# Opening of a retention block: query weights split ahead of key weights, one reduction and one statistics step moved, three fillers taken out

## The reference

```
mod = silu(c) @ wmod              -> sa, ca, ga, sb, cb, gb
ga, gb: sign kept, absolute value at least 0.25
h = layernorm(x) * (1 + ca) + sa
q, k = rotary(h Wq), rotary(h Wk)        8 heads of 64
v = h Wv (8 heads of 128);  g = h Wg
scores = q k^T / 8 * decay, causal;  o = scores v
o = groupnorm(o per head) * w + b, times silu(g);  x = x + ga * (o Wo)
h = layernorm(x) * (1 + cb) + sb
x = x + gb * ffn(h)     r = sigmoid(xr W_r), k = relu(xk W_k)^2, r * (k W_v), with token shift
```

## Time and profile before

| | us |
|---|---|
| median of 3 runs | 750.47 (750.15 to 750.76) |
| the profiled execution | 750.22 |
| its span, first to last instruction | 748.4 |
| TensorE busy | 737.4 |
| VectorE busy | 600.5 |
| GpSimd busy | 589.0 |
| ScalarE busy | 490.2 |

### The profile page before, as it was taken

The page is one execution under the profiler, slowest core; times in us unless marked ns, Lnnn a source line. Parts: engine busy times, 40 slices in busy tenths (PEclk is TensorE's granted clock), DMA queues, the critical chain, the costliest instruction groups (busy, mean ns, idle before and its releaser), DMA issues.

```text
span 748.4 us, 29033 instructions
## 1 busy us (share of the span) xinstructions
PE 737.4 (99%) x12159; PEld 648.3 (87%) x12159; DVE 600.5 (80%) x1265; ACT 490.2 (65%) x956; POOL 589.0 (79%) x643
## 2 busy tenths in 40 slices
PE   8989999999999999999999999999999999999997
PEld 7778888888988888888888988888888988988886
DVE  4997787978788787987879798797987878787546
ACT  4566667676675766767666666756667576656665
POOL 6877788888789887898878888788877988787641
PEclk9999999999999999999999999999999999999999
DMA  6611000001011010111102011020111101001100
GB/s 249 193 31 19 13 17 17 16 18 31 12 27 39 10 44 16 24 37 31 31 10 51 16 24 32 13 48 17 28 26 31 34 14 31 16 9 31 24 16 28
DMA packets 56161, 25.67 MB, mean 34 GB/s; under 512 B 36184, under 2 KB 53856, under 8 KB 56032
## 3 DMA queue, kind: packets, MB, share of 16 engines
q1 hardware_dynamic: 55312, 23.02, 12.9%
q10 hardware_dynamic: 720, 0.80, 0.3%
HBM read 11.22 MB, written 4.20 MB: 21 GB/s over the span
## 4 chain that ended last, share of the span: by engine, by line
PE 92%; DVE 3%; ACT 1%; issue 1%; DMA 1%; POOL 1%; SPq 0%; DVEq 0%
PE ring L309 52%; PE outs L309 15%; PE O_E L309 14%; PE ring L324 8%; PE O_O L309 3%; PE ring L374 2%; DMA N<-in_w_vT 1%; ACT y L771 0%; DVE N L1097 0%; DVE rot_k L1060 0%; DVE A L1070 0%; DVE qT L1031 0%; DVE sin_k L1063 0%; POOL gn_rstd L1383 0%; DVE ln_stats L1004 0%
## 5 line engine op out<-in xcount | busy, mean ns | idle before, releaser
L1390 POOL TENSOR_TENSOR y<-y,gate 128x512 f32<-128x512 f32 x120 | 154.8, 1308 | 29.5 <-ACT y L771 29.5
L735 ACT ACTIVATE v<-ring 64x512 f32<-64x512 f32 x128 | 75.9, 593 | 85.6 <-PE ring L309 84.8
L1373 POOL TENSOR_TENSOR rot_k<-rot_k,sin_k 128x256 f32<-128x256 f32 x128 | 106.8, 856 | 24.1 <-DVE sin_k L1063 24.1
L309 PEld LDWEIGHTS outs<-wo_gated,y 128*128 128x128 f32 x992 | 119.7, 192 | 5.1 <-DVE y L1136 0.5
L309 PE MATMUL outs<-wo_gated,y 128*128 128x128 f32 x992 | 121.7, 275 | 0.1
L1090 DVE TENSOR_REDUCE gn_sum<-N 128x4 f32<-128x512 f32 x118 | 75.5, 681 | 42.4 <-ACT N L759 42.4
L1383 POOL TENSOR_TENSOR gn_rstd<-gn_var,minus_half 128x8 f32<-128x8 f32 x64 | 105.3, 1645 | 5.0
L1070 DVE TENSOR_TENSOR A<-ring,consts 128x256 f32<-128x256 f32 x128 | 47.9, 415 | 60.1 <-PE ring L309 60.1
L771 ACT ACTIVATE y<-ring,gn 128x512 f32<-128x512 f32 x126 | 90.8, 775 | 5.2 <-PE ring L324 5.2
L1367 POOL TENSOR_TENSOR qT<-qT,swapped 128x512 f32<-128x512 f32 x60 | 76.9, 1282 | 18.1 <-DVE swapped L1046 17.8
L743 ACT ACTIVATE kT<-ring 128x512 f32<-128x512 f32 x64 | 38.2, 597 | 80.1 <-PE ring L324 80.1
(11 more groups left out here) (193 smaller groups left out, 2100.8 us busy)
## 6 DMA issues: line engine op xcount, KB each, us to landing
k_odd<-rot_k SPq DMA_DIRECT2D x128, 64.0 KB, 2.4
X<-in_x SPq DMA_DIRECT2D x16, 256.0 KB, 3.9
out<-X SPq DMA_DIRECT2D x15, 256.0 KB, 2.5
key_tables<-in_const SPq DMA_DIRECT2D x7, 256.0 KB, 5.5
rotary_q<-in_const_q SPq DMA_DIRECT2D x2, 512.0 KB, 6.4
gates<-stored_rows SPq DMA_DIRECT2D x8, 128.0 KB, 3.2
N<-in_w_qkT SPq DMA_DIRECT2D x1, 512.0 KB, 5.1
N<-in_w_vT SPq DMA_DIRECT2D x1, 512.0 KB, 6.3
```

The costliest lines, as they stand in the source:

```text
L309: return e.matmul(o, lhsT, rhs, start=start, stop=stop, skip_group_check=True)
L735: done = e.activation(v[halves(half), i % 2, 1, :, :], by(PAIRS, bank_of["v", odd, i][halves(1 - half), :]), ACT.Copy)
L1373: done = e.tensor_tensor(turned[:, n, :, :], turned[:, n, :, :], sin[:, n, :, :], op)
L1390: e.tensor_tensor(y[:, n % NY, :], y[:, n % NY, :], gate[:, n % 2, :], ALU.mult).then_inc(sem["y"])
```

## The change

The one semaphore step of the query and key weights becomes two: ScalarE rounds the query half, then (after the partners) the key half; GpSimd's low parts go in the same order. On VectorE `sum_w_v` moves behind `low_h(0)`. The query pair's own semaphore now comes after three matmuls and the partners' after six; VectorE takes the cosine product first. The last pair's subtraction moves from GpSimd to VectorE. Three fillers ahead of `scores(0)` go. On VectorE `norm_stats(2, 0)` moves behind `rotate_q(6)`; GpSimd's list keeps its order there. The tables of chunks 4 to 7 share one semaphore, which is waited for as a whole.

```diff
 TensorE
-                split_matmul(bank[:, :], [wqk[s][:, cols] ...], h_parts(0))
+                split_matmul(bank[:, :], [wqk[s][:, cols] ...], h_parts(0)).then_inc(sem["proj_q"])
                 at.wait_ge("w_partners_lo", 1)
                 at.wait_ge("sin_q", p - 1)
                 bank = bank_of["q_partners", p] = O[p % 2][:, :, :].rearrange("p n v -> p (n v)")
-                split_matmul(bank, [mix_k[s][:, cols] ...], h_parts(0)).then_inc(sem["proj_q"])
+                split_matmul(bank, [mix_k[s][:, cols] ...], h_parts(0)).then_inc(sem["proj_partners"])
 project_k:
-                at.wait_ge("w_qk_lo", 1)
+                at.wait_ge("w_qk_lo", 2)
             transpose_k(0)
             project_v(1, 1)
-            keep_busy(out_bank, 3, True)
             scores(0)
 ScalarE
-            at.wait_ge("w_qk", 16)
-            split_w("w_qk", raw_qk, wqk)
+            round_w_qk(0)
             norm_apply(0, 0)
             round_w_partners()
+            round_w_qk(1)
+            round_h(0)
             scale_v_mean()
-            round_h(0)
             round_w_v(1)
 VectorE
             norm_stats(0, 0)
-            sum_w_v()
             mod_columns()
             full_h(0)
             low_h(0)
+            sum_w_v()
             rotate_q_pair(0)
...
             add_state(2)
+            rotate_q(6)
             norm_stats(2, 0)
-            rotate_q(6)
             rotate_k(4)
 rotate_q_pair on VectorE:
                 at.wait_ge("proj_q", p + 1)
+                e.tensor_tensor(q, bank_of["q", p][:, :], rotary_q[:, 0, 0:W], ALU.mult).then_inc(sem["cos_q"])
+                at.wait_ge("proj_partners", p + 1)
                 at.wait_ge("qT", p - 1)
+                e.tensor_tensor(partners, bank_of["q_partners", p], rotary_q[:, 1, 0:W], ALU.mult).then_inc(sem["sin_q"])
+                if p == PAIRS - 1:
+                    at.wait_ge("cos_q", PAIRS)
+                    at.wait_ge("sin_q", PAIRS)
+                    e.tensor_tensor(q, q, partners, ALU.subtract).then_inc(sem["qT"])
 GpSimd
-            split_w_qk()
+            low_w_qk(0)
             low_w_partners()
+            low_w_qk(1)
             centre_w_v(1)
...
             rotate_q(2)
-            rotate_q(3)
             rotate_k(1)
```

More of the change, by code:

```diff
@@ L39 @@
 NORM_AHEAD = 4
+EARLY_TABLES = 4
 SEMAPHORES = (
@@ L53 @@
     "silu_c", "sin_k", "sin_q", "small_consts", "sq_E", "sq_O", "state", "sum_E", "sum_O",
-    "swapped", "tables0", "tables1", "tables2", "tables3", "tables4", "tables5", "tables6", "tables7", "v_E",
+    "swapped", "tables0", "tables1", "tables2", "tables3", "late_tables", "v_E",
     "v_O", "v_mean", "v_sum", "w_ffn", "w_g", "w_g_hi", "w_g_lo", "w_k_hi", "w_k_lo",
-    "w_mod", "w_o", "w_qk", "w_qk_hi", "w_qk_lo", "w_v", "w_v_centred", "w_v_hi", "w_partners_hi", "w_partners_lo", "w_v_lo", "wffn_v",
+    "w_mod", "w_o", "w_qk", "w_qk_hi", "w_qk_lo", "w_v", "w_v_centred", "w_v_hi", "proj_partners", "w_partners_hi", "w_partners_lo", "w_v_lo", "wffn_v",
     "wo_gated", "x0", "x1", "x2", "x3", "x4", "x5", "x6", "y", "zero_column",
@@ L257, in outs, with halves_of_w, tables @@
             return [banks[j // PJ][:, j, :] for j in range(GC)]
+        def halves_of_w(n):
+            return slice(n * H * D, (n + 1) * H * D)
         def gates_of(b):
             return "gates%d" % (b % 2), 16 * (b // 2 + 1)
+        def tables(c):
+            return ("tables%d" % c, 16) if c < EARLY_TABLES else ("late_tables", 16 * (CB - EARLY_TABLES))
         def loaded(g):
@@ L348, in project_q_pair @@
                 at.wait_ge("hT_lo", 1)
-                split_matmul(bank[:, :], [wqk[s][:, cols] for s in ("hi", "lo")], h_parts(0))
+                split_matmul(bank[:, :], [wqk[s][:, cols] for s in ("hi", "lo")], h_parts(0)).then_inc(sem["proj_q"])
                 at.wait_ge("w_partners_lo", 1)
@@ L352, in project_q_pair @@
                 bank = bank_of["q_partners", p] = O[p % 2][:, :, :].rearrange("p n v -> p (n v)")
-                split_matmul(bank, [mix_k[s][:, cols] for s in ("hi", "lo")], h_parts(0)).then_inc(sem["proj_q"])
+                split_matmul(bank, [mix_k[s][:, cols] for s in ("hi", "lo")], h_parts(0)).then_inc(sem["proj_partners"])
             def warm_up(n):
@@ L696, in split_w, with round_w_qk @@
                 e.activation(parts["hi"][:, :], raw_w, ACT.Copy).then_inc(sem[name + "_hi"])
+            def round_w_qk(keys):
+                cols = halves_of_w(keys)
+                at.wait_ge("w_qk", 16)
+                e.activation(wqk["hi"][:, cols], raw_qk[:, cols], ACT.Copy).then_inc(sem["w_qk_hi"])
             def scale_v_mean():
@@ L748, in square @@
                 if i < GC:
-                    at.wait_ge(*(("w_partners_lo", 1), ("w_g_lo", 1), ("w_v_centred", 2), ("w_v_lo", 2))[i])
+                    at.wait_ge(*(("w_qk_lo", 2), ("w_g_lo", 1), ("w_v_centred", 2), ("w_v_lo", 2))[i])
                 at.wait_ge("nT_psum", PAIRS * ((i - NN) // GC + 1))
@@ L812, in load_tables @@
                 columns = const[:, n_const + c * H * D:n_const + (c + 1) * H * D]
-                e.dma_start(key_tables[:, c, :, :, :].rearrange("p k h d -> p (k h d)"), columns).then_inc(sem["tables%d" % c], 16)
+                e.dma_start(key_tables[:, c, :, :, :].rearrange("p k h d -> p (k h d)"), columns).then_inc(sem[tables(c)[0]], 16)
             def last_apply(part):
@@ L1024, in rotate_q_pair @@
             def rotate_q_pair(p):
+                q, partners = qT[:, 0, p, :], (turned, swapped)[p % 2][:, :]
                 at.wait_ge("const_q0", 16)
                 at.wait_ge("proj_q", p + 1)
+                e.tensor_tensor(q, bank_of["q", p][:, :], rotary_q[:, 0, 0:W], ALU.mult).then_inc(sem["cos_q"])
+                at.wait_ge("proj_partners", p + 1)
                 at.wait_ge("qT", p - 1)
-                e.tensor_tensor((turned, swapped)[p % 2][:, :], bank_of["q_partners", p], rotary_q[:, 1, 0:W], ALU.mult
-                                ).then_inc(sem["sin_q"])
-                e.tensor_tensor(qT[:, 0, p, :], bank_of["q", p][:, :], rotary_q[:, 0, 0:W], ALU.mult).then_inc(sem["cos_q"])
+                e.tensor_tensor(partners, bank_of["q_partners", p], rotary_q[:, 1, 0:W], ALU.mult).then_inc(sem["sin_q"])
[3 more added lines that the diff above has]
+                    e.tensor_tensor(q, q, partners, ALU.subtract).then_inc(sem["qT"])
             def rotate_q(m):
@@ L1049, in rotate_k @@
                 c, bank = i % CB, bank_of["k", i]
-                at.wait_ge("tables%d" % c, 16)
+                at.wait_ge(*tables(c))
                 at.wait_ge("proj_k", i + 1)
@@ L1321, in norm_rstd, with low_w_qk @@
                                 ).then_inc(sem[f"ln_shift{which}"])
-            def split_w_qk():
-                at.wait_ge("w_qk_hi", 1)
-                e.tensor_tensor(wqk["lo"][:, :], raw_qk, wqk["hi"][:, :].bitcast(F32), ALU.subtract).then_inc(sem["w_qk_lo"])
+            def low_w_qk(keys):
+                cols = halves_of_w(keys)
+                at.wait_ge("w_qk_hi", keys + 1)
+                e.tensor_tensor(wqk["lo"][:, cols], raw_qk[:, cols], wqk["hi"][:, cols].bitcast(F32), ALU.subtract
+                                ).then_inc(sem["w_qk_lo"])
             def low_w_partners():
```

## The result

| | before | after |
|---|---|---|
| median, 6 runs each | 750.17 us | 754.11 us (752.50 to 754.24) |
| the profiled execution | 750.22 | 754.16 |
| its span | 748.4 | 752.4 |

The ratio is 1.0045 (95% interval 1.0034 to 1.0055): slower, and 1.1 us above the forecast range.

The account below looks back on a forecast made before the run. TensorE was taken as the bound, 99% busy, with the opening at VectorE's pace. The statistics move, 1.81 less a 0.48 us lead, gave +1.33 on 750.22: 751.55, or 751.8 as median; forecast 751.5 to 752.1, range 749.9 to 753.0.

Parts of the forecast that it names:

- the lead at the statistics: VectorE, ahead of `norm_stats(2, 0)`: 0.48 us earlier than before, to be taken off the 1.81 us step.
- the clock: Rival: TensorE falls to 1.2 GHz for the twelve projection matmuls behind the new gap; +4.3 us, 754.8; chance 0.05.
- The large term: `norm_stats(2, 0)` behind `rotate_q(6)` delays GpSimd's chain to `norm_heads(1, 0)`: 1.81 less 0.48 of lead, +1.33 us.
- The lead of 1.22 us has shrunk to 0.2 us: VectorE's lead at `low_w_v(1)`, mostly held up by GpSimd's chain and the subtract, leaves 0.2 us at `rotate_k(1)`.
- Lead at that point: 0.48 us: VectorE starts the mask of chunk 2 at 37.24 instead of 37.72; ends 0.2 and 0.75 us.
- 0.4 for a VectorE operation beside it: Opening: GpSimd's key-half subtraction, ending near 12.0, was allowed 0.4 us extra for a VectorE operation beside it.
- a share: GpSimd's extra 0.46 and 0.44 us beside VectorE operations of 0.82 and 0.72 were read as only part of them.
- 752.4 by the rule: Under whole exclusion GpSimd would lose 1.54 us, 0.64 more; the sum becomes 1.33 + 0.64, 752.4 us.
- Edits at nothing: Late tables on one semaphore, `square(0)` waiting for the key half and fewer semaphores: cost 0.
- The other side: Rival: opening lead survives in full, 1.90 us against 1.81, so -0.1 us, 750.4; chance 0.13.

Follow-up runs that it names:

- e5: e1 with GpSimd's low part of the key half made to wait for `hT_lo`; 750.08 us, ratio 0.9990 to the kernel before.
- e7: e1 with `sum_w_v` ahead of `mod_columns` again on VectorE; 750.30 us, ratio 0.9997 to the kernel before.
- e6: e1 with the last pair's subtraction on GpSimd again; 750.29 us, ratio 0.9995 to the kernel before.
- e1: Changed kernel with `norm_stats(2, 0)` back ahead of `rotate_q(6)` on VectorE; 750.91 us, ratio 1.0007 to the kernel before.
- e2: Kernel before with only `norm_stats(2, 0)` moved behind `rotate_q(6)` on VectorE; 753.59 us, ratio 1.0046 to the kernel before.
- e4: Changed kernel with the matmuls of `state(3)` issued three times, giving TensorE work in the gap; 752.81 us, ratio 1.0034 to the kernel before.
- f1: e1 with both GpSimd's key half waiting for `hT_lo` and the last pair's subtraction on GpSimd; 749.52 us, ratio 0.9988 to the kernel before.
- f2: f1 with 5 instead of 9 fillers between the first transposes and `project_q_pair(0)`; 749.42 us, ratio 0.9993 to the kernel before.
- e3: Changed kernel with `head_rstd(1)` ahead of `norm_rstd(2, 0)` in GpSimd's list; 751.30 us, ratio 1.0012 to the kernel before.

## Why the prediction was wrong

Its place and its mechanism of loss were right, its size was not. Two terms failed: the lead at the statistics, forecast as +0.48 us and measured as -0.92, and the clock, which was left out of the sum with a chance of 0.05 and cost 1.45 us. The forecast for one execution was 751.55; with the 1.40 and the 1.45, and 0.2 less for the pause near 75 us, it comes to 754.2, and 754.16 was measured.

- **The large term** held: 1.81 was 1.82, the chain of 3.57 us was 3.57, the idle spot of 2.5 us was 2.43 (before the clock).
- **"The lead of 1.22 us has shrunk to 0.2 us"** failed, with "Lead at that point: 0.48 us". The lead was -1.22 us at `rotate_k(1)` and -0.92 at the statistics. This step failed one part earlier, where GpSimd's key half is allowed "0.4 for a VectorE operation beside it" and `low_h(0)` nothing: I let VectorE always win. It was VectorE that waited, 0.88 us at `low_h(0)` (1.57 against 0.69), 0.74 at `low_w_v(1)` (1.56 against 0.82) under GpSimd's `rotate_q(0)`, of which only the last 0.26 us had lain there before the later centring moved it, and 0.3 more at the gate rows (1.30 against 1.01) under `low_h(1)`. e5 shows the first by taking it away. The second was not taken away by itself, but `low_w_v(1)` took only 0.71 and 0.70 us in the executions of e5 and e7 in which GpSimd's `rotate_q(0)` was nearly over when it started.
- **The -1.22 us in full**: ahead of `low_w_v(1)` the lead was 0.17 (16.03 against 16.20) where 1.22 was forecast, 0.88 of the difference by `low_h(0)` and 0.16 because `full_h(0)` started at 9.16 and not at 9.00. Then come -0.74 in `low_w_v(1)`, +0.14 for the wait ahead of pair 3 that went, and -0.79 for the subtraction and the pause of 0.18 before it. The subtraction had been priced at 0.1, because VectorE was thought to wait for GpSimd there in any case. VectorE was too late for that, and e6 gives 0.82 us at `rotate_k(1)` back.
- **The rule and the row.** The prediction set "a share" against the Trainium skill's whole exclusion (SBUF — State Buffer, "Who interferes with whom"). The trace agrees with the page after all: GpSimd's `rotate_k(0)` began at 16.42 while `low_w_v(1)` ran until 17.02, 0.6 us, and took 0.46 longer. What is lost is the rest of the operation that started first, not the whole of it, and either engine can be the loser. The rows fit this closely, with the loss 0.13 to 0.15 us below the rest: 0.60 gave 0.46, and 0.57 gave 0.44 (GpSimd, before); 1.03 gave 0.88 (`low_h(0)`, after) and 1.17 gave 1.03 (the same in e1); rests of 0.15 and 0.16 gave 0.01 or less (`low_w_v(1)` in e7 and e5, against 0.70 undisturbed). The "752.4 by the rule" priced GpSimd's losses alone. That VectorE can lose stood in the trace before: the last gate product took 1.01 us beside GpSimd's `low_h(1)`, where others of its size took 0.40. The kernel before:

```profile
30.15 0.40 DVE L984 SCALAR_TENSOR_TENSOR gate_rows<-outs,gate_rows 8x256 f32<-8x256 f32 x1
30.59 1.01 DVE L987 TENSOR_TENSOR gate_rows<-gate_pos,gate_rows 8x256 f32<-8x256 f32 x1
30.05 1.27 POOL L1347 TENSOR_TENSOR hT_lo<-h_full,hT_hi 128x512 fp32r<-128x512 f32 x1
```

- **The clock** was a rival with 0.05, priced at +4.3 with the whole twelve projections at 1.2 GHz. It came, with six of the twelve and the transposes behind them slow, and took 1.3 to 1.45 us. Its price in 754.8 was too high, and that the measured 754.11 lies near this rival's time is luck: a price too high met a lead that was not there. The chance was too low because the row it leaned on, no fall across 1.12 us of idle time, says nothing of twice as much: the clock fell after 2.08 us in e2 and 2.39 us in the changed kernel, and not after 0.92 us in e4.
- **Edits at nothing** held: no row after shows a wait for the late tables. The scores of chunk 0 started at 22.68, earlier than before (23.44) but not at 21.5.
- **The other side**, a lead of 1.9 us, had no part in it. Even f1, with one of the blocks taken away and the subtraction back on GpSimd, leads by 0.87 at `rotate_k(1)`.

So the loss of 3.94 us is, by the rows of the profiled execution, 1.8 for the order, 1.45 for the clock and 0.9 for the opening, less the 0.2 us of the pause near 75 us. By the medians the opening is 0.4 (e1). The difference is 0.2 us for the opening of the one execution (`low_h(0)` ended at 12.23 in the changed kernel and at 12.03 in e1), 0.2 us for the same pause, and 0.1 us between profiled executions and medians.

## What to carry to other kernels

Before a step is moved back on one engine, look at the queue of the engine that consumes its result. What stands behind the consumer in that queue waits too; here the statistics held up `head_rstd(1)`, and with it a head norm that does not use them. When VectorE operations with both inputs in SBUF and GpSimd operations are moved, write their new intervals side by side: here the one that started second paid about what was left of the first. And a stall of TensorE can have a second price behind it (here 1.3 us behind a stall of 2.4), so a gap longer than any in the old trace is to be priced with the clock down as well.

## What the runs showed that I had not expected

- TensorE's granted clock was at 0.50 for some microseconds in the opening of several executions (0.60 from 8 to 12 us in the changed kernel, 0.75 in e5, 0.64 and 0.51 in f2 from 8 to 16, 0.61 in e2, 0.64 in e6, 0.50 in e7 from 8 to 12), in others of nearly the same kernel not at all (1.00 in e1, e3, e4 and f1). In the changed kernel TensorE had waited 0.89 us for the constants ahead of it, but 0.74 in e1 and 0.78 in e3, so this does not tell them apart; the cause is open. With nine fillers, most of them at half speed, the first projection came at 12.51 in e5, 0.7 us behind `hT_lo`.
- A VectorE operation of 0.69 us took 1.72 beside a GpSimd one of 1.27 (e1). The reduction `sum_w_v` kept its length beside GpSimd's key half (1.21 us in e5 and in f1), and so did products that read PSUM (0.68 beside GpSimd's `rotate_k(0)` in the changed kernel).
